# A LoRA-augmented NF4 and binary-difference block on one core: gate and up LoRA folded into the weights, a scan with five mean buffers, and fourteen unread matmuls

## What is computed

```python
xn = _layernorm(x, axis=-1)
s = _L0_attn_ref(xn, ...)          # NF4 weights with LoRA
g = _silu(_L0_ffn_ref(xn, ...))    # binary-difference weights
x = x + s * g

# ffn: W = base + mean(|w - base|) * sign(w - base), for each of w1, w2, w3
h = silu(xn @ W1.T) * (xn @ W3.T);   ffn = h @ W2.T

# attn: _lin_lora(x, W, A, B) = x @ W.T + (x @ A.T) @ B.T, W = NF4[codes] * scale per block of 64
x1 = xn + o( (q(xn) + k(xn) + v(xn)) / 3 )
g = _lin_lora(x1, W_gate, A_h[4], B_gu[0])
u = _lin_lora(x1, W_up,   A_h[5], B_gu[1])
s = x1 + _lin_lora(silu(g) * u, W_down, A_down, B_down)
```

## Time and profile before

| | us |
|---|---|
| median of 3 runs | 576.84 |
| lowest, highest | 576.14, 577.93 |
| the profiled execution | 574.28 |
| span of its trace | 572.4 |
| mean granted TensorE clock | 0.985 of full speed |

### The profile page before, as it was taken

The page is one execution under the profiler, slowest core; times in us unless marked ns, Lnnn a source line. Parts: engine busy times, 40 slices in busy tenths (PEclk is TensorE's granted clock), DMA queues, the critical chain, the costliest instruction groups (busy, mean ns, idle before and its releaser), DMA issues.

```text
span 572.4 us, 6430 instructions
## 1 busy us (share of the span) xinstructions
PE 536.3 (94%) x2320; PEld 437.3 (76%) x2320; DVE 430.3 (75%) x493; ACT 334.1 (58%) x453; POOL 104.4 (18%) x110
## 2 busy tenths in 40 slices
PE   0778979999999999999999799999999999999997
PEld 0656868888878788887787588888888888888885
DVE  5988888778885988863569778888768876975335
ACT  2878768555744565443558756868666566555310
POOL 0022303401200220031003120400130031004590
PEclk9979989999999999999999799999999999999999
DMA  8999734213821392058008984861593257327503
GB/s 319 352 367 370 269 135 153 68 58 71 167 84 64 52 219 64 0 120 186 2 0 181 287 152 102 147 145 38 109 176 70 51 101 135 69 57 157 137 18 129
DMA packets 33151, 76.98 MB, mean 134 GB/s; under 512 B 3552, under 2 KB 6496, under 8 KB 32992
## 3 DMA queue, kind: packets, MB, share of 16 engines
q1 hardware_dynamic: 23328, 57.70, 32.6%
q0 software_dynamic: 9792, 18.88, 19.4%
HBM read 53.49 MB, written 2.10 MB: 97 GB/s over the span
## 4 chain that ended last, share of the span: by engine, by line
PE 78%; DVE 9%; DMA 5%; ACT 3%; issue 3%; SPq 1%; POOL 0%; DVEq 0%; ACTq 0%
PE down_ps L1444 24%; PE gate_ps L1416 23%; PE up_ps L1416 22%; PE side_ps L1469 2%; DVE scan_w L952 2%; DMA y<-y_part 2%; PE down_ps L1522 1%; DMA unit_st<-in_mean 1%; DMA xn<-in_x 1%; PE gate_ps L1424 1%; PE up_ps L1424 1%; DMA scan_w<-in_w 1%; PE up_ps L1522 1%; PE gate_ps L1522 1%; DVE xT L993 1%
## 5 line engine op out<-in xcount | busy, mean ns | idle before, releaser
L1416 PE MATMUL gate_ps<-xT,gu 128*128 128x512 f32 x696 | 172.2, 401 | 0.5 <-DVE gu L1018 0.5
L1416 PEld LDWEIGHTS gate_ps<-xT,gu 128*128 128x128 f32 x696 | 135.0, 194 | 30.6 <-DVE gu L1018 1.3
L1444 PE MATMUL down_ps<-h,dn 128*128 128x512 f32 x672 | 156.7, 390 | 0.0
L1416 PE MATMUL up_ps<-xT,gu 128*128 128x512 f32 x624 | 149.2, 390 | 0.7 <-DVE gu L1018 0.7
L1444 PEld LDWEIGHTS down_ps<-h,dn 128*128 128x128 f32 x672 | 126.0, 188 | 27.0 <-ACT y_part L705 0.2
L1416 PEld LDWEIGHTS up_ps<-xT,gu 128*128 128x128 f32 x624 | 117.1, 188 | 26.3 <-DVE gu L1018 1.1
L575 POOL DMA_DIRECT2D y<-y_part x64 | 55.3, 880 | 351.3 <-ACT y_part L705 350.6
L692 ACT ACTIVATE h<-up_ps 128x512 fp32r<-128x512 f32 x52 | 31.0, 597 | 109.9 <-DVE up_ps L1053 56.8
L1141 DVE SCALAR_TENSOR_TENSOR acc<-ramp,acc 128x1536 f32<-128x1536 f32 x42 | 73.7, 1755 | 22.1 <-ACT ramp L756 22.0
L756 ACT ACTIVATE ramp<-codes,bend_bias 128x1536 f32<-128x1536 uint8 x56 | 88.3, 1578 | 0.0
L705 ACT ACTIVATE y_part<-down_ps 128x512 f32<-128x512 f32 x64 | 38.4, 604 | 39.9 <-PE down_ps L1444 35.9
(11 more groups left out here) (172 smaller groups left out, 520.1 us busy)
## 6 DMA issues: line engine op xcount, KB each, us to landing
y<-y_part POOLq DMA_DIRECT2D x64, 256.0 KB, 4.3
scale<-in_scales SPq DMA_DIRECT2D x28, 384.0 KB, 5.5
scan_mean<-in_mean SPq DMA_DIRECT2D x15, 512.0 KB, 6.0
scan_w<-in_w SPq DMA_DIRECT2D x15, 512.0 KB, 6.8
base<-in_mean SPq DMA_DIRECT2D x10, 768.0 KB, 4.5
codes<-in_codes SPq DMA_DIRECT2D x14, 192.0 KB, 5.4
unit_st<-in_w SPq DMA_DIRECT2D x9, 256.0 KB, 6.1
unit_st<-in_mean SPq DMA_DIRECT2D x9, 256.0 KB, 7.2
```

Of the source, the lines that this page charges most:

```text
L1416: last = nc.tensor.matmul(ps[:, :], w[:, w_part, hc * P:(hc + 1) * P], xT[:, x_part, hc, th * HALF:(th + 1) * HALF], start=(hc == 0 and w_ ...
L1444: last = nc.tensor.matmul(down_ps[n % 3][:, :], dn[:, k % DN_SLOTS, w_part, hq * P:(hq + 1) * P], h_part(k, h_p, th), start=(k == ks[0] an ...
```

## The change

**Folded LoRA.** `T`, its copies and the line 1424 go. Instead `rank_gu(k)` multiplies the A and B factors themselves for one chunk, 4 matmuls of 256 columns, into two banks (`gate_pair` in a D stage, `down_pair` in a chunk's stage), and VectorE adds 1024 columns of it to `acc` (`rank_add`) ahead of `lora_add`; `gu_high` then waits for that. `lora_down` moves into the same slot: slot 0 of the stage that splits the chunk, slot 1 in D4. B_gu is laid out by halves of the chunks, and `A_gu` shrinks to 96 rows of 512.

**NF4 steps.** `acc` gets three buffers, four steps move into stage 13, and the counts of the other stages change. The order in stage 13 (`last_ffn_phase`) and in X is new.

**Scan.** `scan_mean` has five buffers, two of them in space of `silu_gate`. `take_coeff` is cut in two (`take_part` first), scan and unit work is reordered on ScalarE and VectorE, and `total(UP)` stands behind all gate projections.

**Unread matmuls.** `fill` issues 8 matmuls 128x512 ahead of `total(GATE)` and 6 behind `total(UP)`; later matmuls overwrite their results.

```diff
-SCAN_W, SCAN_MEAN = 5, 3
+SCAN_W, SCAN_MEAN, MEAN_HOME = 5, 5, 3
+GATE_FILL, UP_FILL = 8, 6
-STAGES = [..., "D3", 13, "X", "D4", "T", 14, 15, 16, "D5", ...]
+STAGES = [..., "D3", 13, "X", "D4", 14, 15, 16, "D5", ...]
-NF4_COUNT = {"X": (4, 0), "D4": (0, 4), 14: (0, 4), 15: (0, 3), 16: (0, 3), "D5": (0, 3), 17: (0, 3),
-             18: (0, 3), 19: (0, 3), "D6": (0, 3), 20: (0, 3), 21: (0, 3), 22: (0, 3), "D7": (0, 3), 23: (0, 3),
-             24: (0, 3), 25: (0, 3), "D8": (0, 2)}
+NF4_COUNT = {13: (0, 4), "X": (4, 0), "D4": (0, 4), 14: (0, 2), 15: (0, 2), 16: (0, 2), "D5": (0, 4), 17: (0, 3),
+             18: (0, 3), 19: (0, 3), "D6": (0, 4), 20: (0, 3), 21: (0, 3), 22: (0, 3), "D7": (0, 4), 23: (0, 2),
+             24: (0, 2), 25: (0, 2), "D8": (0, 2)}
+RANK_ON_GATE = [k for stage, k in SPLIT_IN.items() if k >= B0 and type(stage) is str]
+        LORA_SIDE[stage, 1 if stage == "D4" else 0] = SPLIT_IN[stage]
...
# ScalarE: gu_high, silu, stage 13
-                    act.wait_ge(nf4_scaled, k - B0 + 1)
+                    act.wait_ge(rank_used, k - B0 + 1)
...
+                if k == B0:
+                    act.wait_ge(B_gu_lo, 2)
...
+            def last_ffn_phase(k):
+                steps(k, 0)
+                steps(k, 1, 0, 2)
+                silu(k, 0)
+                MT_high(0, 3)
+                steps(k, 1, 2, 3)
+                MT_high(3, HC)
+                silu(k, 1)
...
# VectorE
+            def rank_add(k):
+                pair = gate_pair if k in RANK_ON_GATE else down_pair
+                gate_up = weight32(k, 0, 2 * HID).rearrange("p (m c n) -> p c m n", m=2, c=HC)
+                dve.wait_ge(nf4_scaled, k - B0 + 1)
+                dve.wait_ge(rank_done, k - B0 + 1)
+                nc.vector.tensor_tensor(gate_up, gate_up, pair.rearrange("p b (c m n) -> p (b c) m n", c=2, m=2), ALU.add
+                                        ).then_inc(rank_used, 1)
...
             def rank_part(stage):
                 if SPLIT_IN.get(stage, 0) >= B0:
+                    rank_add(SPLIT_IN[stage])
                     lora_add(SPLIT_IN[stage])
...
+            def last_ffn_phase(k):
+                steps(k, 1, 0, 1)
+                steps(k, 0, 0, 1)
+                steps(k, 1, 1, 2)
+                steps(k, 0, 1, 2)
+                for c in range(HC):
+                    MT_low(c)
+                h_make(k, 0)
...
# VectorE in X, behind x_low of t
-                        if t == 2:
-                            small_low()
-                        if t == 6:
-                            B_gu_low_rows(GATE)
-                        if t < BENDS - 2:
-                            steps("X", 0, t + 2, t + 3)
+                        if t == 3:
+                            B_gu_low_rows(0)
+                            small_low()
+                            steps("X", 0, 2)
...
# TensorE
+            def fill(bank, count):
+                for _ in range(count):
+                    nc.tensor.matmul(bank[:, :], xT[:, HI, 1, 0:P], xT[:, HI, 0, 0:HALF], start=True, stop=True)
...
-                if k >= B0:
-                    pe.wait_ge(T_lo, th + 1)
-                    pe.wait_ge(B_gu_lo, kind + 1)
-                    c = k - B0
-                    last = nc.tensor.matmul(ps[:, :], B_gu[0:ROWS3, kind, c * P:(c + 1) * P],
-                                            T3[0:ROWS3, th * HALF:(th + 1) * HALF], start=False, stop=True)
...
+            def rank_gu(k):
+                half, at = (k - B0) // 7, (k - B0) % 7 * 2 * P
+                pair = gate_pair if k in RANK_ON_GATE else down_pair
+                if k == B0:
+                    pe.wait_ge(x1_lo, 6)
+                    pe.wait_ge(small_lo, 1)
+                elif k in RANK_ON_GATE:
+                    pe.wait_ge(silu_done, half_count(k - 1, 1))
+                else:
+                    pe.wait_ge(y_out, TT * DOWNS_BEFORE[k])
+                pe.wait_ge(B_gu_lo, half + 1)
+                for hc in range(HC):
+                    last = nc.tensor.matmul(pair[:, hc // 2, hc % 2 * 2 * P:(hc % 2 + 1) * 2 * P],
+                                            A_gu[0:ROWS3, hc * P:(hc + 1) * P], B_gu[0:ROWS3, half, at:at + 2 * P],
+                                            start=(hc % 2 == 0), stop=(hc % 2 == 1))
+                last.then_inc(rank_done, 1)
...
             early_signs(0)
+            fill(gate_ps[1], GATE_FILL)
             total(GATE)
             early_signs(1)
             for c in range(1, FIRST):
                 project(c, GATE, 0)
-                if c == FIRST - 1:
-                    total(UP)
                 project(c, GATE, 1)
+            total(UP)
+            pe.wait_ge(early_part, 2)
+            fill(up_ps[1], UP_FILL)
```

More of the change, by code:

```diff
@@ L138, in block_kernel @@
         scale_qkv = sb("scale_qkv", [P, 4, 3, 8])
+        with nc.sbuf_tensor("acc2", [P, TRIO], f32) as acc2:
+            pass
         sign_rest = sb("sign_rest", [P, 3, SCAN_TILES - 1, 2, HID], i8)
@@ L243, in weight32, with mean_tile @@
         def weight32(k, first, end):
-            return base[:, k % 2, first:end] if k < B0 else acc[k % 2][:, first:end]
+            return base[:, k % 2, first:end] if k < B0 else acc[k % 3][:, first:end]
         def sign_tile(kind, n):
             return sign_first[:, kind] if n == 0 else sign_rest[:, kind, n - 1]
+        def mean_tile(k):
+            slot = k % SCAN_MEAN
+            return scan_mean[:, slot, :] if slot < MEAN_HOME else silu_gate[:, slot - MEAN_HOME + 2, HI, :]
         sign_T = dn[:, 0, HI, :]
@@ L805, in down_stage, with MT_high @@
                         steps(stage, 1, t - 2, t - 1 if t < TT - 1 else None)
-            def MT_high():
-                for c in range(HC):
+            def MT_high(first, end):
+                for c in range(first, end):
                     act.wait_ge(side_used, SIDES - HC + c + 1)
@@ L861, in _ @@
             silu(1, 0)
+            scan_signs(5)
             unit_high(3)
@@ L915, in _ @@
                         nc.scalar.activation(xT[:, HI, hq, sl], x1_ps[t][:, :], ACT.Copy).then_inc(x1_hi, 1)
[L916 removed]
+                        if t == 3:
                             small_high()
[L918 to L925 removed]
+                            steps("X", 0, 2)
+                elif stage == B0 - 1:
+                    last_ffn_phase(stage)
+                    B_gu_scale(0)
+                    B_gu_high(0)
                 elif type(stage) is int:
@@ L1187, in phase @@
                 steps(k, 1, 3)
-                if k == B0 - 1:
-                    MT_low(2)
-                    MT_low(3)
+            def last_ffn_phase(k):
[6 more added lines that the diff above has]
+                h_make(k, 0)
+                steps(k, 1, 2, 3)
+                h_low(k, 0)
+                steps(k, 1, 3)
             def down_stage(g):
@@ L1224, in small_low, with B_gu_low_rows @@
                                         ALU.subtract).then_inc(small_lo, 1)
-            def B_gu_low_rows(kind):
-                dve.wait_ge(B_gu_hi, kind + 1)
-                nc.vector.tensor_tensor(B_gu[64:96, kind, :], B_gu_raw[64:96, 0:INTER],
-                                        B_gu[64:96, kind, :].bitcast(f32), ALU.subtract).then_inc(B_gu_lo, 1)
+            def B_gu_low_rows(half):
+                dve.wait_ge(B_gu_hi, half + 1)
+                nc.vector.tensor_tensor(B_gu[64:96, half, :], B_gu_raw[64:96, 0:INTER],
+                                        B_gu[64:96, half, :].bitcast(f32), ALU.subtract).then_inc(B_gu_lo, 1)
             def early_low():
@@ L1300, in _ @@
             h_make(1, 0)
+            take_part(DOWN)
             h_low(1, 0)
+            h_make(1, 1)
             take_coeff(DOWN)
             unit_make(8)
-            h_make(1, 1)
             unit_make(9)
@@ L1492, in aside @@
                 if (stage, slot) in LORA_SIDE:
+                    rank_gu(LORA_SIDE[stage, slot])
                     lora_down(LORA_SIDE[stage, slot])
+            def rank_gu(k):
[14 more added lines that the diff above has]
+                last.then_inc(rank_done, 1)
             def phase(k):
@@ L1526, in x1_stage @@
                     last.then_inc(x1_done, 1)
-            def rank_stage():
-                pe.wait_ge(x1_lo, TT)
-                pe.wait_ge(small_lo, 1)
-                for th in range(2):
-                    for hc in range(HC):
-                        for a_part, x_part in PASSES:
-                            last = nc.tensor.matmul(up_ps[th][0:ROWS3, :], A_gu[:, a_part, hc, :],
-                                                    xT[:, x_part, hc, th * HALF:(th + 1) * HALF],
-                                                    start=(hc == 0 and a_part == x_part == HI),
-                                                    stop=(hc == HC - 1 and a_part == LO))
-                    last.then_inc(T_done, 1)
             early_mean(0)
@@ L1616 @@
         "B_o": rows_at([(32 * s, B_attn[3].T) for s in range(3)], HID),
```

(4 more changed lines are left out.)

159 lines of the change are left out of this document (73 added, 86 removed).

## The result

| | before | after |
|---|---|---|
| median, us | 576.49 (4 runs, 575.28 to 577.93) | 557.67 (4 runs, 556.84 to 558.15) |
| profiled execution, us | 574.28 | 557.62 |
| span of its trace, us | 572.4 | 555.8 |
| mean granted clock | 0.985 | 0.997 |

The ratio is 0.967 (0.9645 to 0.9697): 18.8 us faster. The prediction was 557.2, range 551.5 to 565. Its sum was made against the profiled execution, though, and there it said 554.7 where 557.62 was measured: 19.6 us forecast, 16.7 found. Before's profiled execution was a quick one, 2.2 us under its own median, and after's was not (0.05 under), so the median was met more closely than the sum deserved: that part of the hit is luck. What follows is about the sum.

A forecast was written before the change was run, and what follows sets the result against it. TensorE's path was taken as the bound: 30.4 us gone less 10.8 come, net 19.6, takes the profiled execution from 574.28 to 554.7; with the median 2.56 above it, 557.2 us, range 551.5 to 565.

The forecast's parts named there:

- Bound and what is removed: On TensorE's path, `T`, 56 LoRA matmuls, the wait behind `T` and its slow clock go: 24.8 us gained.
- 256-column matmuls: 56 new LoRA matmuls on TensorE at 0.12 us each, 0.48 for a chunk: 6.7 us added (6.4 to 12.7).
- small matmuls cost nearly what large ones do: Rival, chance 0.12: the 56 matmuls of 256 columns cost 0.1 us more each, 563 us.
- VectorE's adds: NF4 chunks: 14 adds at 1.14 us, 16 us beside TensorE; 1.0 us booked (0 to 5) at 16, 19 and 22.
- VectorE runs late: Rival, chance 0.15: `h_low` comes 1.5 us after it is wanted at 16, 19 and 22, 4.5 us more, 562.
- 1.3 us (0 to 3.5): D4: `rank_gu(14)` waits for x's low part 6, found ready 0.3 to 2.3 us later than wanted.
- that sign of its own: Wrong above all if D4 and chunk 14 hold a wait long enough that the clock falls again.
- the fourth point: Stage 13, X, D4, chunk 14: MT's 0.7 us wait goes, four steps fit in, new waits add 3.1 us.
- The scan: Stretch up to D0: full clock and five mean buffers start D0 at 79.4 instead of 84.4, gain 4.9 us (2 to 6).
- VectorE then sets the start of D0: End of the scan: coefficient, three makes, lows and h on VectorE take 6.8 us, so D0 starts at 79.4.
- The scan gives back little: Rival, chance 0.12: the clock falls all the same or ScalarE's sums are late; 2 of 4.9 us, 560.
- The new waits don't come: Rival, chance 0.07: the waits of D4 and 14 stay away, 554, or 552 if the scan gives 6.

The follow-up runs named there:

- the padding: Kernel after with an unneeded multiplication by 1 of the same 1024 PSUM columns ahead of each of the 14 `rank_add`: 566.09 us, ratio 0.9826.
- the two moved lines on SyncE: Kernel after with the loads of scale 15 and codes 16 issued ahead of the wait for B_gu's low rows: 552.06 us, ratio 0.9583.

## Why the prediction was right, and where its sum was off

**Bound and what is removed: right.** TensorE's path set the time, and what was taken off it came back almost in full. `T`, its wait and the slow clock behind it are gone.

**256-column matmuls: exact.** They were priced at 0.12 us by the pitch of the transposes' loads. TensorE's groups by shape in after, then the timeline of one chunk:

```profile
L1542 PE MATMUL down_pair<-B_gu,A_gu 96*128 96x256 f32 x36 | 5.8, 283 | 0.0
```
```profile
360.85 0.64 PE L1542 MATMUL down_pair<-B_gu,A_gu 96*128 96x256 f32 x4
361.33 0.40 PE L1514 MATMUL side_ps<-B_down,A_down 96*128 96x512 f32 x1
```

Four take 0.48 us from start to start, though each record is 283 ns long. The rival "small matmuls cost nearly what large ones do" falls. The Trainium skill, "TensorE: Matmul & The Clock Gate", section "Back-to-back issue gap", gives about 131 ns for a sustained matmul of 512 columns. By it the removed matmuls would have been worth 8 us less. It doesn't hold in this kernel: the stretch from chunk 15 to D9 came out as the traced pitch of 0.2275 said.

**VectorE's adds: size exact, place exact, wait smaller.** Timeline of VectorE and TensorE in after:

```profile
375.79 1.21 DVE L1059 TENSOR_TENSOR acc<-acc,down_pair 128x1024 f32<-128x1024 f32 x1
376.92 0.68 DVE L1065 TENSOR_TENSOR acc<-acc,side_ps 128x512 f32<-128x512 f32 x1
...
387.39 5.74 PE L1454 MATMUL up_ps<-xT,gu 128*128 128x512 f32 x24 [0.43 <-DVE h L1080]
```

The pitch of `rank_add` is 1.13 (1.14 forecast). `UP(19, 0)` is the one place in the three groups where TensorE waits for h, 0.43 us; the forecast had it 0.4 early and booked 1.0 for the three. The rival "VectorE runs late" (562) didn't come, but the padding shows its mechanism to be real: with 1.1 us more for each chunk the time was 566.

**Stage 13 and X: right.** X starts without a wait; four steps fit in.

**D4 and chunk 14: the step that failed.** The term "1.3 us (0 to 3.5)" for `rank_gu(14)` measured 3.7, outside its own bounds, and 5.3 with the clock. The prediction had named the scale's DMA as issued only once B_gu's low rows are made, and had seen it late by 1.41 us in the earlier trace rows, but priced the term by VectorE's operations alone, with the DMA landing about in time. What was left out was the landing time behind 672 KB, 8.6 us. The 1.6 us of slow clock were named only as what would make the prediction wrong, and were not in the range of this term. By that sign of its own the fourth point failed, though the total held. Against this, the waits booked for the evictions ahead of `rank_gu(15)` (1.0) and for `gu_low(15)` (0.8) didn't come. In the stretch from X to chunk 15 2.7 were booked and 5.3 came, 2.6 too little, where the stretch missed by 1.7. Most of the other 0.9 is the old wait behind `T`, which cost more than it was priced at. Two more lines of the kernel before, around that wait:

```profile
315.86 2.89 PE L1416 MATMUL gate_ps<-xT,gu 128*128 128x512 f32 x12
...
328.16 0.40 PE L1424 MATMUL gate_ps<-T,B_gu 96*128 96x512 f32 x1
```

The 12.30 us between them hold 24 matmuls and one of the LoRA, 5.7 us at the traced pitches, so the wait and its slow clock were 6.6 and not 6.1 (3.96 and 2.1), 0.5 more. The stretch before also holds three down LoRA matmuls (line 1480) where after's holds two, 0.2 more. `T` took 0.1 us more than its pitch gives, and X 0.1 less in after than before.

**The scan: the sum nearly right, its shares wrong.** 4.5 us against 4.9 (with 4.7 measured for it alone). The clock was full, `total(DOWN)` ran without a wait, and D0 came at 80.98, 79.93 less the late start, against 79.4. But the prediction gave 3.5 us of slow clock to the first wait and the whole closing of the load's hole to the buffers. Runs without either show the order to carry 2.0 to 2.7 us, the unread matmuls about 1 and the buffers 0.5 to 0.7, with executions 1 us and more apart. Its own step "VectorE then sets the start of D0" is why: with VectorE as the bound from 60 to 81 us, a TensorE that is 1.5 us slower just waits less. That step was also mis-sized a little: less the late start `total(DOWN)` began at 72.0, 0.4 before the 72.4 of the forecast, but D0 followed 7.9 us behind it instead of 7.0. Four small waits for h (0.29, 1.00, 0.37 and 0.17) stand in that stretch and were not foreseen.

**Rivals.** "The scan gives back little" (560) falls. "The new waits don't come" (552 to 554) didn't happen here, but the two moved lines on SyncE make it so: 552.06.

## What to carry to other kernels

When an operation gets a DMA as its releaser, price the landing from its issue and from what is queued ahead of it, and look on the issuing queue for semaphore waits that stand in front of it for no reason of its own: two moved lines were worth 5.5 us here, more than the whole rearranged scan. A wait on the bounding engine can cost its slow clock on top (here 1.6 us behind 3.7), but only where that engine goes on being the bound; where it soon waits for another one, keeping its clock up wins nothing. The busy share of a region hides stretches: 80% over the NF4 chunks was 93% in one of them, and padding the suspected engine with one known operation for each chunk shows the room that is left.
